# The attention block and the feed-forward block of a four-stage network put into one block, with the feed-forward's first steps issued among the last score tiles

## Time and profile before

| what | value |
|---|---|
| three runs | 2250.94, 2258.59, 2275.03 us; median 2258.59 |
| the profiled execution | 2256.96 us, its span 2255.2 us, mean granted clock 0.949 |
| busy share of the span | PE 92%, PEld 65%, DVE 67%, ACT 57%, POOL 28% |
| last matmul of the attention ends | 789.35 us from the span's start |
| first matmul of the output projection | 819.95 |
| first hidden matmul of supertile 0 | 850.92 |
| first hidden matmul of supertile 1 | 870.42 |

### The profile page before, as it was taken

How to read it: one execution, slowest core, us unless ns; L and a number is a source line. 1 busy time by engine, 2 the same in 40 slices (tenths; PEclk the granted TensorE clock), 3 DMA queues, 4 the chain that set the end, 5 groups by cost and what they waited for, 6 DMA issues and landing times. The chain is left out here.

```text
span 2255.2 us, 41976 instructions
## 1 busy us (share of the span) xinstructions
PE 2085.5 (92%) x16626; PEld 1476.2 (65%) x16626; DVE 1500.1 (67%) x2406; ACT 1286.7 (57%) x2558; POOL 624.2 (28%) x481
## 2 busy tenths in 40 slices
PE   7999999999999928984999999999999999779998
PEld 6633333333333317973888888888888888658887
DVE  7879999999999438973445454545454544456664
ACT  3248888888888816763444444444444444345654
POOL 1200000000000004532425151515252525224444
PEclk9859999999999969995999999999999999979999
DMA  5822232322220132214203030303030303032321
GB/s 209 242 47 61 65 72 59 80 66 63 67 65 31 35 106 60 71 38 169 90 21 114 20 113 23 111 24 106 10 125 11 127 21 104 10 112 104 113 104 66
DMA packets 95657, 176.77 MB, mean 78 GB/s; under 512 B 19737, under 2 KB 57761, under 8 KB 90337
## 3 DMA queue, kind: packets, MB, share of 16 engines
q1 hardware_dynamic: 95456, 174.03, 25.2%
HBM read 134.54 MB, written 38.67 MB: 77 GB/s over the span
## 5 line engine op out<-in xcount | busy, mean ns | idle before, releaser
L572 DVE TENSOR_REDUCE att_sb_mx<-att_ps_psM 128x1 f32<-128x1024 f32 x512 | 623.9, 1221 | 36.2 <-PE att_ps_psM L605 34.0
L715 ACT ACTIVATE att_sb_pt<-att_ps_psS 128x512 f32<-128x512 f32 x1024 | 557.2, 597 | 92.4 <-PE att_ps_psS L623 37.7
L605 PE MATMUL att_ps_psM<-stack_sb_k,stack_sb_q 48*128 48x512 f32 x1024 | 389.5, 463 | 5.6 <-DVE att_sb_mx L572 4.0
L623 PE MATMUL att_ps_psS<-stack_sb_q,stack_sb_k 50*128 50x512 f32 x1024 | 381.2, 452 | 0.0
L635 PE MATMUL att_ps_psO<-att_sb_pt,stack_sb_v 128*32 128x256 f32 x4096 | 332.6, 397 | 8.6 <-ACT att_sb_osb L708 8.6
L623 PEld LDWEIGHTS att_ps_psS<-stack_sb_q,stack_sb_k 50*128 50x128 f32 x1024 | 157.1, 189 | 206.7 <-ACT att_sb_pt L715 162.1
L635 PEld LDWEIGHTS att_ps_psO<-att_sb_pt,stack_sb_v 128*32 128x32 f32 x4096 | 82.6, 109 | 196.1 <-issue 106.3
L2041 ACT ACTIVATE gla_sb_sg<-gla_ps_psP 128x512 f32<-128x512 f32 x64 | 38.3, 598 | 277.9 <-PE gla_ps_psP L1802 277.9
L2375 POOL TENSOR_TENSOR gla_sb_dm<-gla_sb_dm,gla_sb_masked 128x1024 f32<-128x1024 f32 x64 | 160.4, 2528 | 85.7 <-DMA gla_sb_dm<-decay_rows 85.7
L605 PEld LDWEIGHTS att_ps_psM<-stack_sb_k,stack_sb_q 48*128 48x128 f32 x1024 | 160.3, 193 | 20.9 <-DVE att_sb_mx L572 17.9
L2058 ACT ACTIVATE gla_sb_dm<-gla_sb_dm,gla_sb_neg_g 128x128 f32<-128x128 f32 x512 | 156.4, 391 | 6.0 <-POOL gla_sb_dm L2375 6.0
(11 more groups left out here) (250 smaller groups left out, 4774.1 us busy)
## 6 DMA issues: line engine op xcount, KB each, us to landing
gla_sb_dm<-decay_rows SPq DMA_DIRECT2D x32, 1024.0 KB, 5.6
qk_parts<-stack_sb_part SPq DMA_DIRECT2D x32, 512.0 KB, 3.3
gla_sb_eg<-decay_exp SPq DMA_DIRECT2D x64, 256.0 KB, 6.7
moe_sb_gb<-gate_rows SPq DMA_DIRECT2D x8, 2048.0 KB, 7.1
stack_sb_q<-qk_parts SPq DMA_DIRECT2D x192, 64.0 KB, 2.9
stack_sb_k<-qk_parts SPq DMA_DIRECT2D x96, 128.0 KB, 4.4
att_sb_rb<-sums SPq DMA_DIRECT2D x32, 256.0 KB
attended<-att_sb_on SPq DMA_DIRECT2D x32, 256.0 KB, 4.9
```

Of the source, the lines that this page charges most:

```text
L572: nc.vector.tensor_reduce(mx[:, qh, 8 * r + c:8 * r + c + 1], psM[:, t % 2, :], AX.X, ALU.max).then_inc(maxima_taken, 1)
L605: mm = pe.matmul(psM[:, t % 2, c * ST:(c + 1) * ST], q[rs, g, qh, j, n * P:(n + 1) * P], k[rs, g, j, c * ST:(c + 1) * ST], start=True, sto ...
L623: pe.matmul(psS[:, ring_slot(pos), :], k[rs, g, j, s * P:(s + 1) * P], q[rs, g, qh, j, :], start=True, stop=True).then_inc(ring_done, 1)
L715: nc.scalar.activation(pt[:, s % (LAG + 2), ORDER[i], :], psS[:, (pos + 1) % 3, :], ACT.Exp, scale=AD ** -0.5).then_inc(ring_taken, 1)
```

## The change

- `phase_attention` and `phase_project_ffn` become one function with one block: no barrier and no clearing of semaphores between them.
- `Ffn` no longer takes fresh buffers for all it needs. Class `Area` lays its large tiles at fixed addresses over `part` (weights, made ternary in place: t1 lies on w1 and t2 on w2), over the keys and queries of head groups 0 to 2 (x1, xhi, xlo, h), over `pt` and over the values. PSUM: psT and psA lie in the two maxima buffers, psH in two banks of the score ring, psY in the third and in psO. The transpose uses the attention's `ident`.
- SP issues all weights, biases, xin of supertile 0 and the attended values of supertiles 0 and 1 at the end of body (b, g) = (3, 1), which is within unit 27 (units count from 0 to 31).
- DVE, once its last maximum is taken (in unit 30), sums the weights itself, by a reduction with absolute values in place of ACT's two passes, makes the limits, takes the first two projections, their statistics and both residual additions, shifts xin itself for supertiles 0 and 1, and splits supertile 0 alone (a copy for xhi in ACT's place). The ternary W2 is made inside supertile 0.
- PE makes `project(0)` after the last pairs of unit 30 and the first of unit 31, the sum over partitions in unit 31's step 0, `project(1)` in its steps 2 and 3, and the transposes of supertile 0 after the last pair of its step 6.
- The reciprocal of unit 30 moves behind DVE's split of supertile 0; that of unit 31 behind `split_hidden(0, 0)`. On POOL the norms of supertiles 0 and 1 stand before the multiplication of unit 30, and that of unit 31 stands behind `split_hidden(0, 5)`.
- From supertile 1 on the order is as before, and so are all other stages.

PE in unit 30 and unit 31, before: `att_ps_psS` is a score, `att_ps_psO` values.

The diff, cut to what the text speaks of:

```diff
+class Area:
+    def __init__(self, nc, name, at, end):
+        self.nc, self.name, self.at, self.end = nc, name, at, end
+    def sb(self, name, shape, dt=F32):
+        t = self.nc.alloc_sbuf_tensor_at(f"{self.name}_sb_{name}", shape, dt, offset=self.at)
+        self.at += 4 * int(np.prod(shape[1:]))
+        self.at += -self.at % 32
+        assert self.at <= self.end, (name, self.at, self.end)
+        return t
...
+        part = Area(nc, "ffn", stacks.part_at, stacks.part_at + 32 * kb)
+        keys = Area(nc, "ffn", stacks.k_at, stacks.k_at + 24 * kb)
...
+        in_place = Area(nc, "ffn", part.at, part.end)
+        self.w1, self.w2 = part.sb("w1", [P, KD * FF]), part.sb("w2", [P, FT * D])
+        self.t1, self.t2 = in_place.sb("t1", [P, KD, FF], F32R), in_place.sb("t2", [P, FT, D], F32R)
...
+        self.psT = psM[:, 0, :].rearrange("p (k t) -> p k t", k=KD)
+        self.psA = psM[:, 1, :].rearrange("p (n c) -> p n c", n=NT)
+        self.psH = psSO[:, 0:2, :]
+        self.psY = psSO[:, 2:4, :].rearrange("p b (n c) -> p (b n) c", c=D)
...
+            def ffn_loads():
+                for n, (w, w_t, k) in enumerate(((f_.w1, w1_t, KD), (f_.w2, w2_t, FT))):
+                    sp.dma_start(w[:, :].rearrange("p (k o) -> p k o", k=k),
+                                 w_t.rearrange("(k p) o -> p k o", p=P)).then_inc(f_.w_in[n], 16)
+                sp.dma_start(f_.wo[:, :, :], wo_t.rearrange("(k p) o -> p k o", p=P)).then_inc(f_.first_in, 16)
+                sp.dma_start(f_.b_o[:, :], row(bo)).then_inc(f_.first_in, 16)
+                sp.dma_start(f_.b_h[:, :], b1_cols).then_inc(f_.const_in, 16)
+                sp.dma_start(f_.b_y[:, :], row(b2)).then_inc(f_.const_in, 16)
+                residual_in(0)
+                attended(0)
+                attended(1)
...
+                    if last and qh == 1:
+                        residual_in(1)
+                        for i in range(2):
+                            sp.wait_ge(f_.a_done, i + 1)
+                            attended(i + 2)
...
+                if (b, g) == (BATCH - 1, 1):
+                    ffn_loads()
...
             over_pairs(sp, body)
-            for qh in range(QH):
-                if qh:
-                    sums(2 * NBG - 1, 1)
-                sp.wait_ge(on_ready, 2 * NBG - 1 + qh)
-                out(BATCH - 1, NG - 1, qh)
-            for s in on_out:
-                sp.wait_ge(s, 16 * NBG)
+            sp.wait_ge(on_ready, 2 * NBG - 1)
+            attended_out(BATCH - 1, NG - 1, 0)
+            residual_in(2)
+            sums(2 * NBG - 1, 1)
+            sp.wait_ge(on_ready, 2 * NBG)
+            attended_out(BATCH - 1, NG - 1, 1)
+            for i in range(NST):
+                if i and i + 2 < NST:
+                    residual_in(i + 2)
+                if i > 1:
+                    out(i - 2)
+                if i + 4 < NST:
...
+            def take_turned_first():
+                for k in range(KD):
+                    dve.wait_ge(f_.x_turned, k + 1)
+                    nc.vector.tensor_copy(f_.xhi[:, 0, k, :], f_.psT[:, k, :]).then_inc(f_.xhi_ready, 1)
+                take_turned(0)
...
             over_pairs(dve, body)
-            reciprocal(2 * NBG - 1, 1)
+            nc.vector.memset(f_.ones[:, :], 1.0).then_inc(f_.sums_ready, 1)
+            dve.wait_ge(f_.sums_ready, 1)
+            for n, w in enumerate((f_.w1, f_.w2)):
+                sum_weights(n, w)
+            dve.wait_ge(f_.first_in, N_FIRST)
+            take_projected(0)
+            stats_of_projected(0)
+            limits()
+            below(0, f_.w1)
+            shift_xin(0)
+            dve.wait_ge(ring_done, HG * KT * (2 * NBG - 2))
+            add_projected(0)
+            stats_of_x1(0)
+            ternary(0, f_.w1, f_.t1)
+            normalize_x1(0)
+            take_projected(1)
+            take_turned_first()
+            reciprocal(2 * NBG - 2, 0)
+            stats_of_projected(1)
+            shift_xin(1)
+            add_projected(1)
+            dve.wait_ge(f_.const_in, N_CONST)
+            for i in range(NST):
+                split_hidden(i, 0)
+                if i == 0:
+                    reciprocal(2 * NBG - 1, 1)
+                if i + 1 < NST:
+                    stats_of_x1(i + 1)
+                split_hidden(i, 2)
+                if i > 1:
+                    add_y(i - 2)
+                if i + 1 < NST:
+                    normalize_x1(i + 1)
+                if i:
+                    take_y(i - 1, 0)
+                else:
+                    below(1, f_.w2)
+                    ternary(1, f_.w2, f_.t2)
+                split_hidden(i, 4)
+                if i + 2 < NST:
+                    take_projected(i + 2)
+                    stats_of_projected(i + 2)
+                split_hidden(i, 6)
+                if i + 1 < NST:
+                    take_turned(i + 1)
+                if i:
+                    take_y(i - 1, 1)
+                    stats_of_y(i - 1)
+                if i + 2 < NST:
...
+            def beside_last(u, s, i):
+                if (u, s, i) == (2 * NBG - 2, KT - 2, 3):
+                    pe.wait_ge(maxima_taken, TILES * 2 * NBG)
+                    pe.wait_ge(f_.first_in, N_FIRST)
+                    project(0, range(0, 1))
+                if u == 2 * NBG - 2 and s == KT - 1 and i % 2:
+                    project(0, range(1 + i // 2, 2 + i // 2))
+                if u == 2 * NBG - 1:
+                    if (s, i) == (0, 1):
+                        project(0, range(3, 4))
+                    if (s, i) == (0, 3):
+                        pe.wait_ge(f_.sums_ready, 5)
+                        pe.matmul(f_.psT[:, 0, 0:2], f_.ones[:, :], f_.sums[:, :], start=True, stop=True).then_inc(f_.summed, 1)
+                    if s in (2, 3) and i % 2:
+                        n = 2 * (s - 2) + i // 2
+                        project(1, range(n, n + 1))
+                    if (s, i) == (KT - 2, 3):
+                        turn_x(0)
+            def hidden(i, f):
+                if f == 0:
...
+            pe.wait_ge(f_.w_ready, 1)
+            for i in range(NST):
+                hidden(i, 0)
+                for f in range(1, FT):
+                    hidden(i, f)
+                    if f == FT - 2 and i + 1 < NST:
+                        turn_x(i + 1)
+                    if i:
+                        if i == 1 and f == 1:
+                            pe.wait_ge(f_.w_ready, 2)
+                            pe.wait_ge(osb_ready, 2 * NBG)
+                        y_part(i - 1, (f - 1) // 2, (f - 1) % 2)
+                    if f == 3 and i + 2 < NST:
+                        project(i + 2)
+                if i:
...
     def _(pool):
...
             minus_half(nc, pool, f_.half, f_.half_set)
-            norm_of_projected(0)
-            roots(f_.rs2, f_.stats2, 0, f_.rs2_ready)
-            norm_of_projected(1)
+            split_maxima(0, 0, 0)
+            def body(b, g, last):
+                for qh in range(QH):
+                    start = isinstance(b, int) and b == 0 and g == 0 and qh == 0
+                    if not (last and qh == 1):
+                        split_maxima(*unit_after(b, g, qh))
+                    if last and qh == 1:
+                        norm_of_projected(0)
+                        roots(f_.rs2, f_.stats2, 0, f_.rs2_ready)
+                        norm_of_projected(1)
+                    if not start:
+                        normalize(*unit_before(b, g, qh))
+            over_pairs(pool, body)
             for i in range(NST):
                 split_hidden(i, 1)
                 if i + 1 < NST:
...
+                if i == 0:
+                    normalize(BATCH - 1, NG - 1, 1)
```

622 lines of the change are left out of this document (270 added, 352 removed).

## The result

The changed kernel takes 2223.05 us (median of four runs, 2215.12 to 2234.22), against 2261.53 for the kernel before in the same comparison: a ratio of 0.985, with the interval 0.981 to 0.990. That is faster by 1.5%, in a direction that the prediction had at 0.93. But the time lies 12 us above the 2211 that was forecast, and the execution that was profiled, 2234.22 us with a span of 2232.4, lies 23 us above it. The profiled execution of before has a span of 2255.2, so by the traces 22.8 us are gained where 46.2 were foretold.

The account below looks back on a forecast made before the run. PE, busy 92% of the span, could gain only where it stands still or crawls. Supertile 1 starting 48.2 us earlier, less 2 for the clock, gave 46.2 off 2256.96: 2211 us, range 2202 to 2227 (terms' bounds 2205 to 2217).

Parts of the forecast that it names:

- Step 1: Unit 27: the 4.0 MB of loads delay the sums and DVE stops; 1 us lost, bounds 0 and 4.
- rival (c): Inside attention: the stall in unit 27 drops the clock until attention ends, giving 2278 us; chance 0.03.
- Step 2: Last pairs, units 30 and 31: inserted projection work is partly hidden; 4.4 us lost, bounds 0 and 8.5.
- rival (b): Late DVE chain delays the transposes, all tiles exposed (8.5), loads hold unit 27 up by 4: 2222 us; chance 0.22.
- Step 3: Supertile 0: first hidden matmul at 794.8, DVE waits some 5 us, supertile 1 starts at 822.2, 48.2 us earlier.
- Step 4: Start of supertile 1: PE at 1.2 GHz for about 4 us; 2 us lost, bounds 0 and 2.5.

Follow-up runs that it names:

- e11: Kernel before, no loads added, with two 128x1024 reductions on VectorE behind unit 27's reciprocal; 2262.96 us, ratio 1.004.
- e8: Kernel before, no loads added, with one 128x1024 reduction on VectorE behind unit 27's reciprocal; 2257.22 us, ratio 1.000.
- e1: Changed kernel with its loads in four pieces behind steps of units 25 to 29 instead of 4.0 MB in unit 27; 2213.63 us, ratio 0.982 to before.
- e2: Kernel before with 4.0 MB of loads that nothing reads, at the same place in SP's queue; 2265.07 us, ratio 1.005.
- e3: Kernel before, no loads added, with three 128x1024 reductions on VectorE behind unit 27's reciprocal; 2265.61 us, ratio 1.006.
- e7: Kernel before with eight unread projection-like tiles on TensorE at the changed kernel's places among the last pairs; 2271.24 us, ratio 1.009.
- e10: Changed kernel with loads spread, sums fetched earlier, DVE's order shortened, supertile 2's shift on DVE, POOL kept out of DVE's normalisation; 2200.80 us, ratio 0.978 to before.

## Why the prediction was wrong

**Step 1, the loads: 1 us taken, 21.3 in the trace** (the reciprocal of unit 29 is 19.0 later, that of unit 26 was 2.3 earlier). The transfer was forecast well: the sums landed at 718.95, "at 719". The attention ran 2.3 us early, so DVE waited 3.35 us, within the bounds. What failed is the step from a wait to its price. The prediction priced the wait itself and gave rival (c), the clock, 0.03, since "the stall is 1.5 us, shorter than the 2.91 that left the clock alone". That row was in the feed-forward; that its matmuls are what makes the difference is an argument, not shown. In attention 1.16 us were enough (e11), and with no gap the clock stayed up (e8). Rival (c) had the mechanism and the pace, 2.16 us a pair, but took it to the end of attention, + 54; the clock came back by itself after 44 and 27 us. In the first trace 44 us at 2.16 us a pair instead of 1.23 are 19 us, and with the gap of 2.35 that is about the 21.3. At 0.40 us for each us of low time it is some 11 us on the mean of the runs (e1 against the changed kernel). e2 and e3, with 21 and 25 us of low time more than before, lose some 8 and 10 us by it.

**Step 2, work among the last pairs: 4.4 taken, 9.8 measured** (40.97 us from 777.21 to 818.18, against 31.15), just over the upper bound of 8.5. The prediction let ACT set the pace of a unit and made a room of 0.19 us in each pair by halving the pair of unit 0. There is no room: at full clock a pair is 1.23 us of matmuls without a gap, which is more than half of 2.16. The trace of before had it already (timeline of PE; a pair with maxima, whose matmuls run beside the scores, goes from one L623 to the first of the next pair):

```profile
690.23 0.49 PE L623 MATMUL att_ps_psS<-stack_sb_q,stack_sb_k 50*128 50x512 f32 x1
690.56 0.39 PE L623 MATMUL att_ps_psS<-stack_sb_q,stack_sb_k 50*128 50x512 f32 x1
690.89 0.64 PE L635 MATMUL att_ps_psO<-att_sb_pt,stack_sb_v 128*32 128x256 f32 x8
691.46 0.49 PE L623 MATMUL att_ps_psS<-stack_sb_q,stack_sb_k 50*128 50x512 f32 x1
```

Sixteen such pairs are 19.7 of a unit's 20.25 us, so PE sets the pace. Eight tiles cost 8 x 1.06 = 8.5, and e7 shows it alone. The rest is the transposes and the sum. The transposes were not late, as foreseen (`xn` ready at 807.1, their turn at 812.90), so rival (b) had the exposed tiles right and the reason wrong.

**Step 3, supertile 0: 27.4 taken, 28.3 measured** between the two first hidden matmuls. The wait for `den` was 6.22 us where 5 were foretold, and the normalisation beside POOL took 4.20 us. The prediction took its upper bound, 18.6, from POOL standing in DVE's way, and applied the rule in SBUF — State Buffer, "SBUF: two separate sides", of the Trainium skill to the ternary W2. That took its plain 1.27 and 2.35 us here. It was the normalisation that grew, and e10 shows POOL to be the cause (1.38 alone, 4.20 in the changed kernel beside three of POOL's operations). That agrees with the rule in direction; whether one engine shuts out the other for a whole instruction these rows do not show.

**Step 4, the clock at supertile 1: 2 taken, 2.5 measured** (from supertile 1's first matmul to the transposes for supertile 3 it is 36.86 us, before 34.33). From there on the traces of before and after differ by 1.4 us.

**The sum.** Predicted 46.2 us; in the trace 20.3 are missing by step 1, 5.4 by step 2, 0.9 by step 3, 0.5 by step 4, and 2.3 + 1.4 us of drift before unit 27 and behind supertile 1 come back: 46.2 - 27.1 + 3.7 = 22.8, which is what was gained. On the mean of the runs 28.9 us were gained; there the loads cost 14 (e1 against the changed kernel) and not 1. The forecast's own range, 2205 to 2217, was missed. That the wide one, 2202 to 2227, reaches over the median is luck: it goes that far for rival (b), whose causes (late transposes, a stall of 4 us) were not the ones at work. The profiled execution of 2234 and the second median of this kernel, 2230, lie outside.

## What to carry over

Before a wait is priced, ask what TensorE does behind it: where a gap of a microsecond stood ahead of attention's matmuls, the price was the slower clock that followed, not the gap. Put bulk loads behind small transfers that someone waits for, and in pieces; another queue alone was not shown to help. And read whether an engine has room from its own gaps at the same clock: here scaling its pace from the other level gave 1.08 us for 1.23.
